# Expert stage of a vision tower: gates spread by transfers alone, routing in pairs, the slot stage's outputs placed directly

## What is computed

```python
# slot layer: 64 slots, each with its own fc1, fc2 (gelu between)
y = einsum('sio,bsi->bso', fc1_weight, y) + fc1_bias
y = gelu(y); y = einsum('sio,bsi->bso', fc2_weight, y) + fc2_bias
out = einsum('bsd,bst->btd', y, combine_w)
# expert layer: 8 segments of 16 numbers, 64 experts each, 4 chosen
z = einsum('nd,sdr->nsr', x, P); scores = einsum('nsr,smr->nsm', z, C)
topv, topi = top_k(scores, 4);   w = softmax(topv)
h = gelu(einsum('nsr,nskrh->nskh', z, W1[s, topi]) + b1[s, topi])
yl = einsum('nskh,nskhr->nskr', h, W2[s, topi]) + b2[s, topi]
comb = einsum('nskr,nsk->nsr', yl, w)          # weighted by the gates w
out = gelu(comb @ G1 + g1b) @ G2 + g2b
```

## Time and profile before

| | |
|---|---|
| three runs, median (lowest to highest) | 844.02 us (838.31 to 846.34) |
| the profiled execution, its own time | 839.82 us |
| its span | 838.0 us |
| mean granted TensorE clock | 0.941 |
| busy: PE, DVE, ACT, POOL | 710.7, 510.9, 349.4, 159.2 us |
| slot stage ends, second attention starts | 343.6 us, 359.7 us |
| expert stage, first and last gate product | 561.0 us, 810.7 us |

### The profile page before, as it was taken

How to read it: one execution, slowest core, us unless ns; L and a number is a source line. 1 busy time by engine, 2 the same in 40 slices (tenths; PEclk the granted TensorE clock), 3 DMA queues, 4 the chain that set the end, 5 groups by cost and what they waited for, 6 DMA issues and landing times.

```text
span 838.0 us, 16172 instructions
## 1 busy us (share of the span) xinstructions
PE 710.7 (85%) x6248; PEld 382.8 (46%) x6248; DVE 510.9 (61%) x1291; ACT 349.4 (42%) x597; POOL 159.2 (19%) x199
## 2 busy tenths in 40 slices
PE   5898999899877887579888989979889889979991
PEld 3566676554333343246656665543233323323331
DVE  5578777621111110138687777958978598949876
ACT  0433434142122210023434344346878587838750
POOL 0030403301000000031150405542324032100002
PEclk9899999789889888889999999999999999989996
DMA  7810101439999998831000290564453845456631
GB/s 282 345 45 2 45 2 45 184 123 422 424 419 421 407 402 328 180 107 31 1 29 20 42 118 14 99 215 142 158 158 108 227 134 175 140 180 198 196 112 43
DMA packets 43933, 140.87 MB, mean 168 GB/s; under 512 B 6359, under 2 KB 22299, under 8 KB 39515
## 3 DMA queue, kind: packets, MB, share of 16 engines
q1 hardware_dynamic: 43742, 139.97, 50.3%
q10 hardware_dynamic: 128, 0.05, 0.0%
HBM read 131.91 MB, written 6.18 MB: 165 GB/s over the span
## 4 chain that ended last, share of the span: by engine, by line
PE 46%; DVE 22%; DMA 9%; issue 7%; SPq 5%; ACT 4%; POOL 2%; DVEq 0%; POOLq 0%; ACTq 0%
DMA stream<-in_fc_dram 6%; PE P L2155 5%; PE P L2116 5%; PE P L376 5%; DVE work L2259 4%; SPq L2049 3%; PE P L849 3%; PE P L448 2%; PE P L858 2%; PE P L2128 2%; PE P L891 2%; PE P L419 2%; ACT work L2220 2%; PE P L866 2%; PE P L1360 2%
## 5 line engine op out<-in xcount | busy, mean ns | idle before, releaser
L2220 ACT ACTIVATE work<-P 128x768 f32<-128x768 f32 (+1 forms) x192 | 149.4, 828 | 52.2 <-PE P L2116 52.1
L2259 DVE TENSOR_TENSOR work<-work,early 128x768 f32<-128x768 f32 (+1 forms) x96 | 98.0, 1021 | 20.2 <-DMA early<-gate_dram 10.6
L2116 PE MATMUL P<-early,stream 99*128 99x384 bf16 (+1 forms) x384 | 98.6, 340 | 10.4 <-ACT work L2220 10.2
L2259 DVE TENSOR_TENSOR work<-work,P 128x768 f32<-128x768 f32 (+1 forms) x96 | 93.3, 972 | 23.2 <-PE P L2128 20.4
L2155 PE MATMUL P<-work,stream 128*32 128x384 f32 (+1 forms) x768 | 97.0, 514 | 4.0 <-DVE work L2259 3.5
L530 ACT ACTIVATE work<-work 101x444 f32<-101x444 f32 x48 | 28.1, 586 | 114.4 <-DVE work L525 114.4
L2116 PEld LDWEIGHTS P<-early,stream 99*128 99x128 bf16 x384 | 29.1, 98 | 92.9 <-ACT work L2220 61.5
L943 DVE COPY work<-P 128x768 f32<-128x768 f32 x16 | 15.3, 956 | 91.6 <-PE P L875 91.6
L626 POOL TENSOR_SCALAR work<-work 101x4 f32<-101x4 f32 x12 | 2.7, 228 | 349.5 <-DVE work L616 349.5
L927 ACT ACTIVATE work<-P 128x768 f32<-128x768 f32 x16 | 13.0, 811 | 126.4 <-PE P L866 126.4
L2128 PE MATMUL P<-early,middle 96*128 96x384 bf16 (+1 forms) x192 | 49.4, 339 | 11.7 <-DMA early<-stream 8.2
(11 more groups left out here) (262 smaller groups left out, 1233.9 us busy)
## 6 DMA issues: line engine op xcount, KB each, us to landing
stream<-in_fc_dram SPq DMA_DIRECT2D x14, 2304.0 KB
early<-gate_dram SPq DMA_DIRECT2D x64, 384.0 KB, 3.4
stream<-in_fc_dram SPq DMA_DIRECT2D x15, 1536.0 KB, 8.9
early<-gate_dram SPq DMA_DIRECT2D x32, 416.0 KB, 4.2
stream<-in_fc_dram SPq DMA_DIRECT2D x15, 768.0 KB, 10.4
early<-in_patches_dram SPq DMA_DIRECT2D x4, 888.0 KB, 5.3
stream<-w_dram SPq DMA_DIRECT2D x6, 512.0 KB
stream<-in_fc_dram SPq DMA_DIRECT2D x2, 1152.0 KB
```

The lines of the kernel that those rows point to most:

```text
L2116: mm = pe.matmul(P[:, j, 0:WIDE[c]], w1s[:, seg, (hh * (CH // 2) + i) * 128:(hh * (CH // 2) + i + 1) * 128], zs[c][:, seg, :], start=True, ...
L2220: act.activation(act_out[p % 4][:, :, 0:cols], P[:, 2 * x:2 * x + 2, 0:cols], ACT.Gelu_apprx_tanh).then_inc(s_ua, 1)
L2259: dve.tensor_tensor(gated[:, at:at + 2, 0:cols], act_out[p % 4][:, :, 0:cols], by, ALU.mult).then_inc(s_ug, 1)
```

## The change

1. **Gates.** `gate_pair`, `parts`, `stage_gates` and the bf16 copies are gone. Gates are kept once in f32 (`gates`), stored tile by tile, and one transfer per unit spreads the gates of all four segments (twice the bytes). DVE multiplies a unit by one instruction of 4 x 384 (or 416) instead of two. The b2 bias is two f32 products instead of one f32 and six bf16.
2. **Buffers.** The hidden pairs use three pairs of banks (0 to 5) in turn, `act_out` holds three units, the spread gates four units (one place of the ring lies in `work` and can be filled only after the last layer norm of the second attention).
3. **Routing.** Tiles 3 to 9 go in pairs (3,4), (5,6), (7,8), 9, by a table of steps; both tiles' exponentials stand together between one pair of table loads. The second tile has buffers of its own.
4. **Slot stage.** `y_dram` is laid out by image parity, so a group is stored by two transfers, and a gathered slot is one run of 12 KB instead of 16 runs of 768 B. The last two groups are placed directly (`place`): group 14 by 8 transfers on ACT, group 15 by 4 on SP and 4 on ACT.

```diff
-        def place_last(eng, js):
-
-            eng.wait_ge(s_yo, GROUPS)
+        def place(eng, g, js):
+
+            eng.wait_ge(s_yo, g + 1)
...
             gather(GROUPS - 4, 0, SLOTS - 4 * GS)
+            gather(GROUPS - 2, SLOTS - 4 * GS, SLOTS - 2 * GS)
             sp.wait_ge(s_hid, GROUPS)
...
-            store(GROUPS - 2)
-            gather(GROUPS - 1, SLOTS - 4 * GS, SLOTS - GS)
-            place_last(sp, (0, 1))
+            place(sp, GROUPS - 1, (0, 1))
...
-            place_last(act, (2, 3))
+            place(act, GROUPS - 2, range(GS))
+            place(act, GROUPS - 1, (2, 3))
...
-        BEGINS = {3: 10, 4: 18, 5: NG + 5, 6: NG + 14, 7: 2 * NG + 9, 8: 2 * NG + 18, 9: 3 * NG + 5}
...
+        BEGINS = {3: 10, 5: NG + 5, 7: 2 * NG + 9, 9: 3 * NG + 5}
+        STEPS = ("scores", "take", "top_a", "top_b", "mark_a", "mark_b", "exps", "shares", "select", "turn", "gates")
+        TIMES = (dict(zip(STEPS, (0, 2, 3, 4, 7, 8, 10, 11, 13, 14, 17))),
+                 dict(zip(STEPS, (3, 4, 5, 6, 9, 10, 10, 12, 15, 16, 19))))
...
                 if g % NG == 0:
-                    sp.wait_ge(s_gd, 32 * (1, 4, 8)[c])
-                if g >= RING:
-                    sp.wait_ge(s_ug, 2 * (g - RING) + 2)
+                    sp.wait_ge(s_gd, 32 * (3, 6, TT)[c])
+                if HOME[g] in HOME[:g]:
+                    sp.wait_ge(s_ug, max(x for x in range(g) if HOME[x] == HOME[g]) + 1)
+                elif HOME[g] == 3:
+
+                    sp.wait_ge(LO["h_out"], QP * QUADS)
                 row = 32 * hh + 4 * i
-                src = gate_dram[c][sq, row:row + 4].rearrange("r k t -> r (k t)")
...
+                src = gate_dram[c][row:row + 4, sq].rearrange("r b k t -> r (b k t)")
...
-            store_gates(0, 2)
-            stage_chunk(0)
+            for t in range(FIRST):
+                store_gates(t)
...
-            def gate_pair(g):
...
-                for j in range(2):
-                    mm = pe.matmul(P[:, 4 + j, 0:WIDE[c]], gate_sel[:, i, :], ws[c][:, 4 * sq + 2 * j + hh, :],
-                                   start=True, stop=True)
-                mm.then_inc(s_bc, 1)
...
+            def gate_unit(g):
+                cols = WIDE[g // NG]
+                dve.wait_ge(s_ua, 2 * g + 2)
+                dve.wait_ge(s_sg[HOME[g]], landed(g))
+                if g >= 2:
+
+                    dve.wait_ge(s_u2, g - 1)
+                at = 4 * (g % 2)
+                dve.tensor_tensor(gated[:, at:at + 4, 0:cols], act_out[:, 4 * (g % 3):4 * (g % 3) + 4, 0:cols], spread_gates(g),
+                                  ALU.mult).then_inc(s_ug, 1)
```

315 lines of the change are left out of this document (125 added, 190 removed).

## The result

The changed kernel took 846.38 us (median of 12 runs, 835.68 to 851.84), the kernel before 843.03 us beside it (829.69 to 851.23). The ratio is 1.0078, interval 1.0043 to 1.0113: slower by 0.8%, where I had said 813 us. (Ratios leave out executions more than 1.5% above the fastest of their kernel.) A second comparison gave 1.0063 (1.0025 to 1.0101). An unchanged copy of the kernel before measured 1.0041 (0.9993 to 1.0090) against itself, so part of these 0.6 to 0.8% may be the measurement's; what is sure is that nothing of the forecast 3.6% came.

The account below looks back on a forecast made before the run. DVE was taken as nearest bound, PE hardly behind. Work 202, loops 8, transfers 14, chunk starts 8.5 and 2 make 234.5 us; 18.7 plus the slot stage's 10 off 839.8 gave 811, stated as 813, range 800 to 832.

Parts of the forecast that it names:

- I keep 8 us of such waits in all: Expert stage: DVE's remaining waits on the loop through PE and ACT, 8 us, from 0 to 31.
- The slot stage: End of the slot stage: store, wait and gather leave the path, `combine` near 350 us, 10 us saved.
- from the last issue to `combine` I take the 2.9 us of now: End of the slot stage: `combine` follows ACT's last transfer issue by 2.9 us, as before, so starts at 350.0.
- at the 421 GB/s of the earlier trace its 1.2 MB take 3 us: Slot stage: the large gather in 12 KB runs takes 3 us, where 768 B runs held the queue 8 us.
- The start of the expert stage: First chunk: the first gated product starts at 558.5 us instead of 561.0.
- DVE's work: Expert stage: one 4 x 384 or 416 product per unit, 1.67 or 1.81 us, cuts DVE's work to 202 us.
- The transfers: Expert stage: spread gate loads become the new bound; waits of 14 us, 8.5 at chunk starts, 2 for the fourth load.
- So the loop closes with 0.27 us to spare: Expert units: the loop through PE and ACT takes 3.35 us against 3.62 us of two DVE products.
- What PE and ACT insert for routing has to fit beside DVE's own: Expert stage: routing work on PE and ACT must fit beside DVE's routing; no separate size given.
- TensorE's clock: I give it no case of its own: Expert stage: a lower clock while PE stands still gets no separate case; any effect is inside the first rival's time.
- slower, by one mechanism, loads at 295 GB/s: Expert stage: spread loads run at 295 GB/s throughout and pace all units; 850 us, chance 0.05.
- My first rival: Loops stay tight or small slot-stage transfers queue behind the weights; 8 to 10 us less gain, 822 us, chance 0.20.

Follow-up runs that it names:

- the quarters: Changed kernel with the large gather of the slot outputs cut into eight loads with 3072 B runs instead of two with 12288 B; ratio 0.9919.
- one tile at a time: Changed kernel with tiles 3 to 9 routed one after the other at the old places, each with its own exponentials; ratio 1.0069.
- Half loads: Changed kernel with most spread gate loads of chunks one to three bringing two of four segments, so the output differs; ratio 0.9856.
- one filler: Changed kernel with one added product of zeros on TensorE per expert unit, ahead of the expert output; ratio 1.0073.
- four fillers: Changed kernel with four added products of zeros on TensorE per expert unit, ahead of the expert output; ratio 1.0437.
- both: Changed kernel with half of most spread gate loads and gelus cut to 192 columns together; 815.78 us, median of 4 executions, no interval.
- no tables: Changed kernel with the exponentials of tiles 3 to 9 replaced by a scaled copy, so ACT never changes its table in the expert stage; ratio 1.0044.
- TensorE kept at work: More filling products ahead of the second attention's `combine`: 15 instead of 4 in the changed kernel, ratio 1.0005; 18 in the kernel before, 1.0112.
- short gelus: Changed kernel with most gelus covering 192 of the 384 or 416 columns, so the output differs; ratio 1.0109.
- three fillers behind: Changed kernel with three added products of zeros on TensorE per expert unit, behind the expert output; ratio 1.0323.
- slot end taken back: Changed kernel with the old store, gather and placings at the end of the slot stage; ratio 1.0031, 839.42 us.
- rows later: ACT's gelu of the output rows moved behind the second gelu of its unit: changed kernel, ratio 1.0064; kernel before, ratio 1.0015.
- new slot end and rows later: Kernel before with the new end of the slot stage and the later gelu of the output rows together; ratio 0.9958, median 837.14 us.

## Why the prediction was wrong

The profiled execution took 37 us more than the 811 that the sum gave for it. 18 of them are in the expert stage (252.4 for 234.5), 14 in the second attention, for which no change was forecast (212.5 for some 199), 3 in `combine`'s start (353.2 for 350.0) and 2 in the end. The step that failed in the expert stage is the term "I keep 8 us of such waits in all".

**The slot stage: 10 us said, 5 came.** `combine` starts at 353.4 us in the mean of thirteen profiles with the new end (351.2 to 357.4), at 358.1 in four with the old one; the two with added fillers ahead of it are left out. The step that failed is "from the last issue to `combine` I take the 2.9 us of now": it is 8.4. Behind it failed "at the 421 GB/s of the earlier trace rows its 1.2 MB take 3 us": the gather ran at 155 GB/s, took its 7 us as before, and the placings, issued in good time, stood in the queue behind it and behind the four weight loads, which landed at 347.1 to 351.4. The 2.9 us of the earlier trace rows belong to a queue that had run empty. Where the last copy comes late and the queue has time to drain, they are nearly right: with the copy at 345 us or later it is 1.8 to 5.7 us, with it at 343.1 or earlier 4.2 to 9.5, and `combine` comes at about the same time either way. I had blamed the 768 B runs for the slow queue of the earlier trace rows (1.39 MB in 8 us, 174 GB/s); the quarters show that the run's length hardly counts there. One transfer that fills both halves at once was not tried. The rule of the Trainium skill that I had weighed ("DMA: Bandwidth & Descriptors", Rules for kernel authors: many small transfers cost mostly overhead) gave me "a few us"; that size was right. Its reason is not shown here: the engines were held by the gather's large packets and the weights.

**The start of the expert stage: 2.5 us said, 2 came.** Between `combine` and the first product kernels of the new kind need 2 us less at the same clock (table below).

**DVE's work: 209 to 202 said, 209.5 to 204.7 came.** The product is 1.76 us long with 384 columns and 1.89 with 416, and two in a row start 1.67 and 1.80 us apart, as said. Of the 2.7 us more, three `select`s account for most (1.5 instead of 0.7 us), and seven products take 2.0 to 2.6. I put this down to GpSimd, which works for two tiles at these places; it fits that with one tile at a time DVE had 4.5 us less to do.

**The transfers: 24.5 us of waits said (14 in the run, 8.5 at the chunk starts, 2 for the fourth load), 21.8 came,** 2.4 of them ahead of the first product. The unit's period in the last chunk, 2.0 to 2.2, was right, the rate too (365 GB/s at 0.94 of the engines, so 388 at full), and the waits at the starts of chunks two and three are 2.6 and 3.2 us, with smaller ones behind them. Half loads give 16.7 us back.

**The loops: 8 us said, 26 came** (24.2 for PE and ACT, 1.5 for GpSimd). This is the step that failed, and not where it was worked out. "So the loop closes with 0.27 us to spare" was for two units, 0.14 for one; measured at full clock it is 0.15 (1.65 to 1.80). What failed is what stood behind it without a sum. Two things were left out of it.

The first is in "What PE and ACT insert for routing has to fit beside DVE's own". PE works through its program in order, and so does ACT. A product of PE that is not a unit's own (the bias products 1.5 us, `out_hidden` 1.5, a tile's scores 1.1, a turn 0.7; by their groups 7.5 + 3.0 + 7.9 + 7.5 = 26 us of PE in the stage) and each of ACT's copies, sums and exponentials pushes the loop back by its length. With 0.15 us a unit it would take ten units to catch up 1.5 us; this is worked out, no row shows a lead being won back.

The second is in "TensorE's clock: I give it no case of its own". The loop was added up from rows at full clock. At half clock it takes 3.05 us and doesn't close at all. 58 of the stage's 252 us ran so, where it had been 17 of 251, and there or within 4 us behind stand 17.0 of the 24.2 us of waits for PE and ACT (in the five profiles with this stage unchanged 12.6 to 19.5 of 21.0 to 25.4). Outside them 7.2 us are left, close to the 8 that I had kept, where the kernel before had 18.8: so at full clock the waits did go, and half clock brought others. How much of the 17 us is the clock's is not shown. Transposes and output rows, which delay the loop at any clock, stand in the same places; where one unit could be compared it was 0.9 us of 3.8, and six units later nothing of it was left.

So the waits did not go with the gate products: of 31.1 us for PE and ACT 24.2 stayed. I had counted the 20.4 us behind PE's last product, the gate product, as caused by it, because it was the last to end; what stood in front of it in PE's queue delayed the expert output as well.

The parts add up: 204.7 us of work, 19.4 for transfers inside the stage, 24.2 for PE and ACT, 1.5 for GpSimd and 2.6 in gaps too short for the list make 252.4. And the two kinds of wait hide each other: 57 us less on ACT give 4.7, and 5.7 us of waits taken from the output rows give nothing, for the load behind them would have been late. In the last chunk the unit was 2.00 us by PE's gate products and is 2.0 by the loads: there the change moved the bound from an engine to the queue and left it in place. I had set the loads' 2.13 us against DVE's 1.81 and never against the 2.00 that stands in the earlier trace rows.

**TensorE's clock.** In the timed runs the mean clock of the changed kernel was 0.89 to 0.918, of the one before 0.917 to 0.953. Three stretches have to be told apart.

In the expert stage the fall belongs to the change (0.86 to 0.93 in all fourteen profiles with the new stage, 0.94 to 0.97 in the five with the old). What it costs there is open. The five profiles with this stage unchanged show no order (0.86: 254.0 us, 0.87: 250.1, 0.88: 249.3, 0.89: 252.4 and 252.0), one filler brought 0.92 and 252.1, but none has more than 0.93, so what the clock of before would give isn't measured.

Behind it the end takes 26.9 to 30.6 us instead of 26.3, in the mean 2.6 us more: this is the change's.

In the second attention it costs much:

| kernel | clock | second attention, us |
|---|---|---|
| new expert stage: four fillers, quarters | 0.99 | 198.5, 199.8 |
| both, no tables | 0.98 | 199.0, 200.3 |
| TensorE kept at work, short gelus | 0.96 | 202.6, 202.5 |
| one tile, half loads, three fillers behind | 0.94 | 205.8, 204.4, 204.6 |
| slot end taken back | 0.92 | 209.0 |
| changed twice, one filler, rows later | 0.91 | 212.5, 211.0, 211.6, 211.1 |
| old expert stage: before | 0.99 | 201.3 |
| before again, TensorE kept at work | 0.98 | 201.9, 201.6 |
| rows later | 0.97 | 203.0 |
| new slot end and rows later | 0.91 | 214.8 |

The same products, 14 us apart: 0.18 x 212.5 = 38 us at half clock against 0.02 x 198.5 = 4, so about 0.4 us for each us at half, as the expectations had it. A clock of 0.92 or less stands there in one of the five profiles with the old stage and in five of the fourteen with the new. So it needs neither the new expert stage nor the new slot end. Whether the new expert stage makes it more frequent, these few profiles can't tell, and what decides it in one execution and not in the next stays open.

**The chances.** I had 0.05 for slower, by one mechanism, loads at 295 GB/s. Loads ran at 388. My first rival named the right causes (loops that stay tight, or small transfers that queue, with the clock inside it) and gave them 8 to 10 us, 0.20. It was 18 us in the loops alone, 5 of the slot stage and 2.6 of the end on top: the mechanism was there, the size was half or less.
